# SRC pass of a two-layer graph network: a new order of ScalarE and VectorE steps, and TensorE's turns, pair sums and products of a group made in blocks

## What is computed

```python
h = x @ Wn.T + bn                                    # layer 0: attention over edges, then segment_sum by dst
x = _layernorm(x + relu(out0))
agg = segment_sum(x[nbr], dst1); mean = agg / maximum(count, 1)      # layer 1, with dst1 = src, nbr = dst
x = _layernorm(x + x @ W1.T + b1 + mean @ W2.T + b2)
```

## Time and profile before

| | us |
|---|---|
| median of three runs | 1405.91 |
| lowest and highest of them | 1404.85, 1406.67 |
| the profiled execution's own time | 1415.9 |
| its span, first to last instruction | 1414.1 |

### The profile page before, as it was taken

One profiled execution on the slowest core, in us unless ns is written; L12 is line 12 of the kernel. 1 busy time (PEld: TensorE's weight loads), 2 busy tenths in 40 slices (PEclk: granted clock), 3 DMA queues, 4 the chain that ended last, 5 costly groups with the idle time before them and its releaser, 6 DMA issues.

```text
span 1414.1 us, 25043 instructions
## 1 busy us (share of the span) xinstructions
PE 1201.5 (85%) x6829; PEld 1046.3 (74%) x6829; DVE 1002.8 (71%) x3483; ACT 745.4 (53%) x1743; POOL 751.7 (53%) x731
## 2 busy tenths in 40 slices
PE   5988968991099999949999999999988888888884
PEld 5977857880078888838888888888877777777773
DVE  8377897989455555349999999999985556555551
ACT  3754664550034444427777766667674544545442
POOL 1047772777767777744444106555541555555533
PEclk9989999996589999979999999999998889988887
DMA  6868887979436666657777768999961323222211
GB/s 213 272 150 206 208 225 184 272 231 348 171 68 93 101 94 92 72 137 246 239 240 245 248 241 296 310 321 325 325 238 51 91 94 94 86 91 88 93 47 43
DMA packets 118160, 254.11 MB, mean 180 GB/s; under 512 B 23705, under 2 KB 63272, under 8 KB 118084
## 3 DMA queue, kind: packets, MB, share of 16 engines
q1 hardware_dynamic: 75738, 187.26, 41.8%
q0 software_dynamic: 40128, 64.45, 20.1%
q10 hardware_dynamic: 2218, 1.53, 0.3%
HBM read 175.67 MB, written 130.44 MB: 216 GB/s over the span
## 4 chain that ended last, share of the span: by engine, by line
PE 70%; DVE 11%; DMA 6%; ACT 5%; issue 5%; POOL 1%; SPq 0%; DVEq 0%; ACTq 0%; POOLq 0%
PE bank L1389 41%; PE bank L1378 8%; PE bank L1366 5%; DVE stats L971 4%; PE bank L1438 3%; PE bank L1288 3%; PE bank L1442 3%; DMA X<-in_x,idx_src 3%; DVE X L798 2%; ACT aggn L633 2%; PE bank L1533 2%; ACT sel L687 1%; PE bank L1325 1%; DVE xT L801 1%; DVE xin L798 1%
## 5 line engine op out<-in xcount | busy, mean ns | idle before, releaser
L1389 PE MATMUL bank<-w1T,xT 128*128 128x256 f32 x1968 | 480.3, 392 | 2.0 <-ACT yout L596 2.0
L1389 PEld LDWEIGHTS bank<-w1T,xT 128*128 128x128 f32 x1968 | 378.0, 197 | 56.6 <-ACT xT L586 3.0
L494 POOL DMA_INDIRECT order_scratch<-pay,rank_i x200 | 194.6, 973 | 220.6 <-DVE xin L798 90.3
L586 ACT ACTIVATE xT<-bank 128x512 f32<-128x512 f32 x296 | 176.7, 598 | 91.5 <-PE bank L1378 87.0
L596 ACT ACTIVATE yout<-bank,rstd 128x256 f32<-128x256 f32 x492 | 203.8, 480 | 0.7 <-DVE rstd L1037 0.5
L591 ACT ACTIVATE std<-stats,eps_c 128x4 f32<-128x4 f32 x271 | 80.5, 298 | 230.5 <-DVE stats L971 230.4
L534 POOL DMA_INDIRECT z_scratch<-xin,idx_out x100 | 156.3, 1563 | 53.8 <-ACT xin L713 30.6
L971 DVE BATCH_NORM_STATS2 stats<-bank 128x6 f32<-128x512 f32 x246 | 167.9, 691 | 10.2 <-PE bank L1389 10.1
L971 DVE BATCH_NORM_STATS2 stats<-xin 128x6 f32<-128x512 f32 x240 | 154.6, 686 | 22.6 <-DMA xin<-z_scratch 22.6
L1389 PE MATMUL bank<-w2T,xT 128*128 128x256 f32 x400 | 126.7, 446 | 50.4 <-ACT xT L586 41.8
L487 POOL DMA_INDIRECT out_rows<-yout,idx_out x100 | 102.4, 1024 | 107.7 <-ACT yout L596 83.0
(11 more groups left out here) (249 smaller groups left out, 1765.7 us busy)
## 6 DMA issues: line engine op xcount, KB each, us to landing
z_scratch<-in_x SPq DMA_DIRECT2D x125, 400.0 KB
xin<-z_scratch SPq DMA_DIRECT2D x97, 512.0 KB, 4.8
out_rows<-yout SPq DMA_DIRECT2D x97, 512.0 KB, 3.7
kB<-sorted_scratch SPq DMA_DIRECT2D x50, 256.0 KB, 3.4
yout<-low_digits_scratch SPq DMA_DIRECT2D x50, 128.0 KB
yout<-keys_scratch SPq DMA_DIRECT2D x50, 128.0 KB, 5.7
yout<-in_edge_attr SPq DMA_DIRECT2D x12, 512.0 KB, 6.2
order_scratch<-pay,rank_i POOLq DMA_INDIRECT x200
```

Source lines behind the costliest of these rows:

```text
L494: g.indirect_dma_start(out=order_dram[k], out_offset=bass.IndirectOffsetOnAxis(ap=rank_i[k][:, t:t + 1], axis=0), in_=pay[:, t, :], in_off ...
L586: a.activation(xT[dst_i][:].rearrange("p a b c -> p (a b c)"), src_bank[:, :], ACT.Copy, bias=raised).then_inc(copied, 1)
L1389: ins = mm(to, buf[:, jj, c, 0:n], w[:, c, :], start=not bias and i == 0 and c == 0, stop=i == len(terms) - 1 and c == 1)
```

## The change

On TensorE a step makes the turns of both pairs, then the sums of both, then the products of both. On ScalarE the root of the own moments moves one group ahead (group q + 1 in step q, group 0 before the loop); the step begins with the copy of pair 0 and the normalising of group q's own rows; both roots follow, then the output rows of pair 0 of group q - 2, the copy of pair 1, the output rows of pair 1, and last the neighbours' weighing and root. On VectorE the own moments and offsets move one group ahead too, through the new functions `own_stats` and `own_offsets`; the step begins with the moments of the products of group q - 2, and the carry stays last. The number of instructions that do work stays as it was.

The core of the diff:

```diff
@@ ScalarE @@
+            root(0, s_ost, 1, s_osq)
             weigh_neighbours(0, 0)
...
-                if in_range(q, 0, Q):
-                    root(u % 2, s_ost, q + 1, s_osq)
+
+                def last_step(p):
+                    if in_range(q, 2, Q + 2):
+                        y_rows(0, (u - 2) % 4, 2 + u % 2, s_ey, lambda b: rbank(u % 2, b), P, (2 * p, 2 * p + 1))
                 own_copy(0)
-                if in_range(q, 2, Q + 2):
-                    root(2 + u % 2, s_est, q - 1, s_esq)
-                own_copy(1)
                 if in_range(q, 0, Q):
                     act.wait_ge(s_onm, q + 1)
...
+                if in_range(q, 2, Q + 2):
+                    root(2 + u % 2, s_est, q - 1, s_esq)
                 if in_range(q, 0, Q - 1):
-                    weigh_neighbours(q + 1, u + 1)
-                if in_range(q, 0, Q - 2):
-                    root_neighbours(q + 2, u)
+                    root((u + 1) % 2, s_ost, q + 2, s_osq)
                 if in_range(q, 2, Q + 2):
                     hu = (u - 2) % 4
                     act.wait_ge(s_enm, q - 1)
...
-                    y_rows(0, hu, 2 + u % 2, s_ey, lambda p: rbank(u % 2, p))
+                last_step(0)
+                own_copy(1)
+                last_step(1)
+                if in_range(q, 0, Q - 1):
+                    weigh_neighbours(q + 1, u + 1)
+                if in_range(q, 0, Q - 2):
+                    root_neighbours(q + 2, u)
@@ VectorE @@
+            def own_stats(q, m, u):
+                own = own_rows(q, u)
+                dve.wait_ge(s_xs[u % 4], 16 * GT * (m + u // 4 + 1))
+                moments(u % 2, lambda p: own[:, 2 * p:2 * p + 2, 0:D], P, s_ost)
+
+            def own_offsets(q, m, u):
+                slot = u % 2
+                dve.wait_ge(s_osq, q + 1)
+                invert(slot, P, n_m[slot] + counted(m, u, 0, 2) + 1)
+                stt(nmr[:, slot, :], stats[:, slot, :, 1], -1.0, rstd[:, slot, :], ALU.mult, ALU.mult).then_inc(s_onm, 1)
+
+            own_stats(0, 0, 0)
+            own_offsets(0, 0, 0)
+
             def by_src(q, m, u):
                 slot = u % 2
-                if in_range(q, 0, Q):
-                    own = own_rows(q, u)
-                    dve.wait_ge(s_xs[u], 16 * GT * (m + 1))
-                    moments(slot, lambda p: own[:, 2 * p:2 * p + 2, 0:D], P, s_ost)
-                if in_range(q, 0, Q - 1):
-                    select_src(q + 1, m, u, 1)
...
                 if in_range(q, 2, Q + 2):
                     dve.wait_ge(s_er, 2 * (q - 2) + 2)
                     moments(2 + slot, lambda p: halves(rbank(slot, p)[:, :]), P, s_est)
-                if in_range(q, 0, Q - 2):
-                    neighbour_stats(q + 2, u)
+                if in_range(q, 0, Q - 1):
+                    own_stats(q + 1, m, u + 1)
                 if in_range(q, 2, Q + 2):
                     dve.wait_ge(s_esq, q - 1)
                     v.reciprocal(rstd[:, 2 + slot, :], std[:, 2 + slot, :]).then_inc(s_enm, 1)
+                if in_range(q, 0, Q - 1):
+                    select_src(q + 1, m, u, 1)
+                    own_offsets(q + 1, m, u + 1)
+                if in_range(q, 0, Q - 2):
+                    neighbour_stats(q + 2, u)
                 if in_range(q, 0, Q):
                     sums_with_carry(q, u)
@@ TensorE @@
-                for p in range(2):
-                    if in_range(q, 1, Q + 1):
+                if in_range(q, 1, Q + 1):
+                    for p in range(2):
                         pe.wait_ge(s_ex1, GT * h + 2 * p + 2)
...
-                    if in_range(q, 0, Q):
-                        pe.wait_ge(s_sel[SRC], q + 1)
+                if in_range(q, 0, Q):
+                    pe.wait_ge(s_sel[SRC], q + 1)
+                    for p in range(2):
                         wait(pe, s_carry, 8 * h + 4 * p + 4)
...
-                    if in_range(q, 1, Q + 1):
+                if in_range(q, 1, Q + 1):
+                    for p in range(2):
                         pe.wait_ge(s_carry, 8 * h + 4 * p + 4)
```

More of the change, by code:

```diff
@@ L1229, in _ @@
             n_m = [G // 2 + (i % 2 < G % 2) for i in range(4)]
+            def own_stats(q, m, u):
[9 more added lines that the diff above has]
+            own_offsets(0, 0, 0)
             def by_src(q, m, u):
                 slot = u % 2
-                if in_range(q, 0, Q):
-                    own = own_rows(q, u)
-                    dve.wait_ge(s_xs[u], 16 * GT * (m + 1))
-                    moments(slot, lambda p: own[:, 2 * p:2 * p + 2, 0:D], P, s_ost)
-                if in_range(q, 0, Q - 1):
-                    select_src(q + 1, m, u, 1)
-                if in_range(q, 0, Q):
-                    dve.wait_ge(s_osq, q + 1)
-                    invert(slot, P, n_m[slot] + counted(m, u, 0, 2) + 1)
-                    stt(nmr[:, slot, :], stats[:, slot, :, 1], -1.0, rstd[:, slot, :], ALU.mult, ALU.mult).then_inc(s_onm, 1)
                 if in_range(q, 2, Q + 2):
```

## The result

The changed kernel takes **1321.03 us** (median of four runs), against 1405.38 for the kernel before beside it. The ratio is 0.9387, with a 95% interval of 0.9353 to 0.942. Forecast were 1317 us and 1310 to 1338: the time lies in the range, 4 us over the forecast. A few executions were disturbed and stand in no ratio: one of the four here took 1364.76 us and one of experiment 2 1382.76 (the medians count both; that of the other three here is 1319.70), and two of experiment 3 took 1360.75 and 3159.70.

What follows compares the result with a forecast made beforehand. TensorE was taken to pace the kernel, losing 3.80 us a step to one wait and the clock drop behind it. Steps -87.4 and last step -1.4 gave -88.8, to 1327.1; less 10 for the median, 1317 us, range 1310 to 1338.

Steps and rivals of the forecast that it cites:

- 23 steps: SRC pass, turn of step 2 to that of step 25: 13.62 us a step becomes 9.82, -87.4 us.
- low end: 1310 us: the start's -2, and 0.2 us a step less for fewer switches between kinds of matmul (-5).
- rival (a): GpSimd paces the SRC pass's end, its issues lengthened by VectorE's selections: 1323 us, or 1330 with two long issues; chance 0.18.
- The gathers' margin: SRC pass, GpSimd: falls behind TensorE 0.54 us a step, 9.7 over 18 steps; a margin of 12 just does not bind.
- the tight place: ScalarE's copy of pair 1, behind normalising, both roots and two rows: lands at 5.5 us, wanted at 6.27, 0.8 to spare.
- signs of being wrong: SRC pass: regular TensorE wait for the second copy, clock at 0.50, VectorE waiting early for gathered rows, steps of 10.4 or more.
- The selections: SRC pass: a GpSimd issue meeting a VectorE selection takes 0.4 us more; by the skill's rule every step would pay.
- The layout of the step: One SRC step timed from TensorE's first turn on three engines with the old distances: 9.82 us if nothing is waited for.
- (b): SRC pass: copy of pair 1 late by hand-overs 1.5 us later, TensorE waits 0.7 a step: 1334 us; chance 0.10.
- (c): SRC pass: copy of pair 1 so late that the 2 us wait and clock drop return: 1406 us, half-way 1360; chance 0.06.
- (d): SRC pass: GpSimd's gathers and scatters without a pause run at 1.56 us, 15.3 a step: slower, 1418 us; chance 0.04.
- The clock: TensorE in the SRC pass: granted clock stays at 1.00 with no wait left; waits of a few tenths cost themselves alone.

Runs made afterwards that it cites:

- experiment 2: Changed kernel with ScalarE's and VectorE's order as before, only TensorE's order new: 1338.99 us, ratio 0.9515 to the kernel before.
- experiment 3: Changed kernel with GpSimd's gathers issued one scatter earlier, from group 14 on two: 1319.19 and 1320.73 us, no ratio.
- experiment 1: Changed kernel with TensorE's order as before, only ScalarE's and VectorE's order new: 1323.60 us, ratio 0.9413 to the kernel before.
- experiment 4: Changed kernel with seven small memsets on GpSimd behind each gather from group 7 on: 1327.98 us, ratio 0.9434 to the kernel before.
- experiment 5: Changed kernel with the root of the products' moments ahead of copy 0 on ScalarE: 1344.58 us, ratio 0.9544 to the kernel before.
- experiment 6: Changed kernel with the root of the own moments ahead of copy 0 on ScalarE: 1394.65 us, ratio 0.9897 to the kernel before.
- the two repeats: The changed kernel run again unaltered, beside the experiments: 1319.69 and 1317.59 us, ratios 0.9379 and 0.9359 to the kernel before.

## Why the prediction was right, point by point

| part of the span | forecast | measured |
|---|---|---|
| stages ahead of the SRC pass (first sums 1056.26, now 1053.45) | 0 | -2.8 |
| start, first sums to the turn of step 2 (15.42, now 14.50) | 0 (-2 to +2) | -0.9 |
| 23 steps (313.33, now 224.94) | -87.4 | -88.4 |
| last step (9.93, now 8.52) | -1.4 | -1.4 |
| tail (19.2, now 19.2) | 0 | 0 |
| sum | -88.8 | -93.5 |

The -2.8 us ahead of the pass is no effect of the change, which touches nothing there: in the eight other traces with these stages unchanged (experiments 1 to 6 and the two repeats) the first sums begin between 1047.56 and 1055.29.

**The steps** came out right by two errors of opposite sign, which is luck. A step without late rows is 9.57 us, not 9.82: 23 x 0.25 = 5.8 us better. The prediction had that only at its low end, as 0.2 a step for fewer switches. Experiment 1 names part of it: with the sums of both pairs between turn and products, the first products' weights are loaded under the sums. And the margin of the gathers did bind, by 4.4 us in steps 19 to 23: rival (a), in its place and near its size ("the last 6 lose about 1 each"), though brought on by the shorter TensorE step more than by the long issues that (a) names. Some 0.4 more lies in single longer steps.

**The gathers' margin** is the step that failed. The deficit of GpSimd was forecast as 10.36 - 9.82 = 0.54 us a step, and 9.7 in all was to fit into some 12. The rows, from the gather of group 6, the first behind a scatter, to that of group 20, the first to come late, and TensorE's turns in the steps that want their moments:

```profile
1081.69 1.43 POOL L484 DMA_INDIRECT xin<-z_scratch,idx_src  x1 [0.30 <-issue]
...
1227.84 0.98 POOL L484 DMA_INDIRECT xin<-z_scratch,idx_src  x1 [0.30 <-ACT yout L596]
```

```profile
1096.65 1.04 PE L1393 MATMUL bank<-ident,xin 128*128 128x128 f32 x8
...
1231.10 1.04 PE L1393 MATMUL bank<-ident,xin 128*128 128x128 f32 x8
```

GpSimd took 146.15 us for 14 steps, 10.44 each (10.30 where no issue is long), and TensorE 134.45, 9.60 each: 0.84 a step, 11.7 us in all. So the margin of 12 was right and GpSimd's pace nearly so; the TensorE step of 9.82 in the deficit was the term that was too long, and 18 steps at 0.84, 15 us, do not fit into 12. The late rows reach TensorE through the copy of pair 1, the tight place that the prediction named. Where it expected no wait over 0.3 us, there are 0.60, 0.77, 0.72 and 0.92, and steps of 10.4 and more, one of its signs of being wrong, came four times.

**The selections** that GpSimd meets were a price in rival (a), and the trace shows when it is paid: when the issue begins while a selection is running.

```profile
1206.94 0.69 DVE L1069 TENSOR_TENSOR csel<-kB,prevk 128x512 f32<-128x512 f32 x1
...
1279.03 0.68 DVE L1071 TENSOR_TENSOR sel<-kB,keyc 128x512 f32<-128x512 f32 x1
1279.12 1.45 POOL L487 DMA_INDIRECT out_rows<-yout,idx_out  x1 [0.30 <-issue]
```

The scatter at 1279.12 begins with 0.59 us of a selection left and takes 1.45; the gather at 1206.85 (above), under way when a selection begins, takes 0.99. In the changed kernel's SRC pass the 11 issues that begin with 0.31 to 0.59 us of a selection left take 1.17 to 1.45, that rest and 0.82 to 0.88 more; none that begins with no selection running takes over 1.04. Nine are longer than 1.2 us now and six were before (the earlier trace rows shows one). Four of the nine lie in steps 20 to 23, one in each: VectorE's `sel` there follows the late moments by the same 2.16 us, and so meets the same scatter each time. GpSimd's step is 10.6 us there (these scatters begin at 1247.24, 1257.89, 1268.50 and 1279.12), close to the 10.8 of rival (a). The Trainium skill's rule on shared interfaces ("GPSIMD Engine Reference", Key points) agrees with the issues that begin under a selection; that every step would pay, as the prediction took it, came true in the late steps alone.

**The layout of the step** held to 0.2 us. After the step's start: copy 0 lands at 1.33 (forecast 1.22) and is wanted at 2.66, the root of the own rows begins at 4.04 (3.89), copy 1 lands at 5.54 (5.5) and is wanted at 6.12 (6.27). VectorE is free for 1.4 to 1.6 us (1.9) and ScalarE for 2.36 (2.5). Of rivals (b) and (c) nothing is seen before the gathers come late, and of (d) nothing: gathers and scatters without a pause keep their 0.98 and 1.02 us.

**The clock** stayed up, as forecast, and waits of 0.6 to 1.1 us cost themselves alone in every kernel here (the changed one, experiments 2, 4 and 5).

**The median** is 4 us over the forecast (2.7 without the run of 1364.76) though the trace gained 5 us more than forecast. The profiled execution before, from which the terms came, was 10 us over the median, at a mean clock of 0.925; seven others of that kernel, beside the first three experiments, took 1402.95 to 1410.66 at 0.927 to 0.935. The forecast took these 10 us off both kernels alike, but the changed kernel's profiled run is only 1 to 3 us over its median, so part of the terms was a loss that the median run does not have. The lower mean clock says that some of it was time at the lower level, and experiment 6 makes the SRC pass a likely place, since there the same wait loses the clock in some steps and not in others. Some of it may lie ahead of the pass, which began later in that trace (1056.26) than in any other here. The unprofiled runs have no trace, so the shares stay open.

## What to carry to other kernels

On an engine that works in order, look for an instruction that needs another engine's late result and stands ahead of one that is ready and waited for: here the new order of two engines, with no work added, took a step from 13.62 us to 9.80 (experiment 1), nearly half of that through the clock. Then lay the new step out against every engine that does not wait, and work out its deficit against the shortest step that could come out, not the step in the records: a queue that is 9% too slow (10.44 against 9.60) looks free for most of the pass and binds in the last five steps with gathers. Two cures for the same wait do not add; measure each alone before keeping both.

## What the runs showed of the hardware that was not expected

- A wait of TensorE of about 2 us does not always lose the clock. In the kernel before it did in 22 of 23 steps, in experiment 6 in 11 of 22, and waits of the same length did both (2.14 us at 1199.52 and at 1252.31 in experiment 6). Waits up to 1.1 us never lost it in a step here. The Trainium skill ("TensorE: Matmul & The Clock Gate", Part 1: The HAM clock gate) says that the chip's watch on activity runs free and is not started by a kernel's work; by that, where a wait falls would count beside its length. The equal waits with unequal ends agree with it, but no run here moved such a wait on purpose, so it is not shown.
- An indirect DMA's issue on GpSimd that begins 0.09 us or more into a selection of VectorE (two inputs of 128x512), with 0.3 or more of it left, takes that rest and 0.82 to 0.88 us (one that began 0.04 us into one, at 1158.93, took its usual 0.95); a selection that begins 0.09 us or more into an issue runs its usual 0.68 or 0.69 us, and the issue is no longer than others either.
- Seven memsets of 128x4 on GpSimd took 0.31 us, and the gap ahead of the next indirect DMA shrank from 0.30 to 0.16 us: a small instruction between two issues costs less than its own time.
- The first weight load behind a change of operand is hidden when the copy that the products wait for is there early: 0.87 us for four products where it ended 1.33 us ahead of them, 0.97 where it ended 0.12 ahead.
